# An eight-layer linear-attention block with a mixture of ten units, one Trainium2 core: the mixture's down product in plain f32

## What is computed

```python
scores = jax.nn.softmax(xf @ router_w, axis=-1)
topk_scores, topk_idx = jax.lax.top_k(scores, TOP_K)
combine = jnp.zeros((N, E), dtype=x.dtype).at[jnp.arange(N)[:, None], topk_idx].add(topk_scores)
g = jnp.einsum('nh,ehf->enf', xf, gate_w)
u = jnp.einsum('nh,ehf->enf', xf, up_w)
y = jnp.einsum('enf,efh->enh', jax.nn.silu(g) * u, down_w)
routed = jnp.einsum('enh,ne->nh', y, combine)
shared = jax.nn.silu(xf @ shared_gate_w) * (xf @ shared_up_w) @ shared_down_w
x = x + gb * (shared + routed)
```

## Time and profile before

| | |
|---|---|
| runs | 521.98, 522.12, 523.74 us, median 522.12 |
| profiled execution | 523.33 us, its span 521.3 us |
| PE busy | 505.4 us, 97% of the span |
| DVE, ACT, POOL busy | 425.6, 404.2, 294.5 us |
| granted PE clock, mean | 0.993 |
| the mixture, steps 2 to 39 | 414.8 to 517 us of the span |

### The profile page before, as it was taken

One profiled execution on the slowest core, in us unless ns is written; L12 is line 12 of the kernel. 1 busy time (PEld: TensorE's weight loads), 2 busy tenths in 40 slices (PEclk: granted clock), 3 DMA queues, 4 the chain that ended last, 5 costly groups with the idle time before them and its releaser, 6 DMA issues.

```text
span 521.3 us, 8267 instructions
## 1 busy us (share of the span) xinstructions
PE 505.4 (97%) x1993; PEld 310.4 (60%) x1993; DVE 425.6 (82%) x1631; ACT 404.2 (78%) x606; POOL 294.5 (56%) x328
## 2 busy tenths in 40 slices
PE   8789999999999999999999999999989999899997
PEld 6445555555555555555555555555555568687885
DVE  5879888988898888888888988888886667877754
ACT  3848888888888888888888888888887866657552
POOL 4435655556656566655566555666545567555652
PEclk8989999999999999999999999999999999999999
DMA  8200010001000000100010001001000000000000
GB/s 242 97 16 1 7 41 15 0 5 40 15 5 20 20 15 5 41 15 0 5 40 15 5 4 36 15 5 29 12 1 1 2 0 1 21 1 21 2 21 20
DMA packets 16070, 11.22 MB, mean 22 GB/s; under 512 B 8220, under 2 KB 13852, under 8 KB 16052
## 3 DMA queue, kind: packets, MB, share of 16 engines
q1 hardware_dynamic: 15188, 10.29, 7.1%
q10 hardware_dynamic: 864, 0.73, 0.5%
HBM read 9.96 MB, written 1.05 MB: 21 GB/s over the span
## 4 chain that ended last, share of the span: by engine, by line
PE 84%; DVE 6%; POOL 4%; issue 3%; ACT 2%; DMA 1%; DVEq 0%; POOLq 0%; ACTq 0%
PE bank L436 19%; PE bank L427 15%; PE bank L302 12%; PE bank L449 6%; PE bank L424 5%; PE bank L344 4%; PE bank L349 4%; PE bank L345 4%; PE bank L546 3%; PE bank L548 3%; PE bank L547 3%; PE bank L591 1%; PE bank L594 1%; PE bank L592 1%; PE bank L606 1%
## 5 line engine op out<-in xcount | busy, mean ns | idle before, releaser
L436 PE MATMUL bank<-hid,wf 128*128 128x512 f32 x256 | 120.2, 592 | 0.0
L917 POOL TENSOR_TENSOR rsD<-veD,c_half 128x4 f32<-128x4 f32 x32 | 37.3, 1166 | 100.7 <-DVE veD L1031 100.7
L427 PE MATMUL bank<-x,wf 128*128 128x512 f32 x192 | 93.9, 598 | 0.0
L755 ACT ACTIVATE hid<-bank,vbf 128x512 f32<-128x512 f32 x128 | 77.6, 694 | 1.9 <-PE bank L427 1.9
L436 PEld LDWEIGHTS bank<-hid,wf 128*128 128x128 f32 x256 | 46.0, 190 | 46.6 <-issue 30.8
L1002 POOL TENSOR_TENSOR xs_lo<-sc,xs_hi 128x512 fp32r<-128x512 f32 x36 | 46.6, 1296 | 41.4 <-ACT xs_hi L875 41.3
L427 PEld LDWEIGHTS bank<-x,wf 128*128 128x128 f32 x192 | 35.4, 191 | 33.7 <-issue 16.5
L1121 DVE TENSOR_SCALAR x<-bank,vln 128x256 f32<-128x256 f32 x64 | 31.9, 540 | 23.8 <-PE bank L302 23.8
L1050 DVE TENSOR_SCALAR xhB<-bank,meanB,rsB 128x128 f32<-128x128 f32 x128 | 43.8, 407 | 9.2 <-POOL rsB L917 9.2
L1050 DVE TENSOR_SCALAR xhD<-bank,meanD,rsD 128x128 f32<-128x128 f32 x128 | 43.7, 406 | 7.4 <-POOL rsD L917 3.2
L725 ACT ACTIVATE g<-bank,vbf 128x512 f32<-128x512 f32 x31 | 21.4, 691 | 35.5 <-PE bank L436 35.5
(11 more groups left out here) (173 smaller groups left out, 1178.7 us busy)
## 6 DMA issues: line engine op xcount, KB each, us to landing
wf<-in_w_f SPq DMA_DIRECT2D x16, 256.0 KB, 2.7
wu<-in_w_unit SPq DMA_DIRECT2D x10, 192.0 KB
wqkv<-in_w_qkv SPq DMA_DIRECT2D x7, 192.0 KB, 2.3
x<-in_x SPq DMA_DIRECT2D x4, 256.0 KB, 5.5
out<-ot SPq DMA_DIRECT2D x3, 256.0 KB, 2.2
wo<-in_w_o SPq DMA_DIRECT2D x8, 64.0 KB, 1.8
wmod<-in_w_mod ACTq DMA_DIRECT2D x1, 256.0 KB, 5.6
vln<-in_v_ln SPq DMA_DIRECT2D x16, 1.0 KB, 1.7
```

The costliest lines, as they stand in the source:

```text
L427: mm = nc.tensor.matmul(ps_ff[j][:], wf1[:, j * P:(j + 1) * P], x2[(c - 2) % CH][:], start=True, stop=True)
L436: mm = nc.tensor.matmul(ps_f0[:], wf2[:, j, :], hid[:, j, :], start=(j == 0), stop=(j == FJ - 1))
L755: nc.scalar.activation(hid[:, j, :], ps_ff[j][:], ACT.Gelu_apprx_tanh, bias=vbf1[:, j:j + 1]).then_inc(h_ready, 1)
L917: nc.gpsimd.tensor_tensor(rs[buf(k, n)][:], ve[buf(k, n)][:], c_half[:], ALU.pow).then_inc(rstd_ready[k], 1)
```

## The change

The down product of every step is one plain f32 matmul of `wu` and the unit's result `sc` itself. `sc_hi`, `sc_lo`, ACT's rounding, POOL's subtraction, `splits` and the waits that belong to them go. `wu_hi` and `wu_lo` are made for the gate and up matrices only (128x256 in place of 128x384). POOL's last four weight parts, which stood behind the low parts of steps 2, 4, 5 and 7, stand at steps 2 to 5. The slots that drain the layers keep their order.

```diff
-                if splits(i + 1) == splits(i):
-                    unit_done(pe, i)
-                    mm = nc.tensor.matmul(ps_y[:], wu[:, u, 2, :], sc[i % 3][:], start=(u == 0), stop=(u == U - 1))
-                else:
-                    k = splits(i)
-                    pe.wait_ge(sc_hi_ready, k + 1)
-                    nc.tensor.matmul(ps_y[:], wu_hi[:, u, 2, :], sc_hi[k % 2][:], start=(u == 0), stop=False)
-                    nc.tensor.matmul(ps_y[:], wu_lo[:, u, 2, :], sc_hi[k % 2][:], start=False, stop=False)
-                    pe.wait_ge(sc_lo_ready, k + 1)
-                    mm = nc.tensor.matmul(ps_y[:], wu_hi[:, u, 2, :], sc_lo[k % 2][:], start=False, stop=(u == U - 1))
+                unit_done(pe, i)
+                mm = nc.tensor.matmul(ps_y[:], wu[:, u, 2, :], sc[i % 3][:], start=(u == 0), stop=(u == U - 1))
...
-                    nc.scalar.activation(wu_hi[:, u, :, :], wu[:, u, :, :], ACT.Copy).then_inc(wu_hi_ready, 1)
+                    nc.scalar.activation(wu_hi[:, u, 0:2, :], wu[:, u, 0:2, :], ACT.Copy).then_inc(wu_hi_ready, 1)
...
-                if splits(i) > splits(i - 1):
-
-                    k = splits(i - 1)
-                    unit_done(act, i - 1)
-                    if k >= 2:
-                        act.wait_ge(down_mm, i - 2)
-                        act.wait_ge(sc_lo_ready, k - 1)
-                    nc.scalar.activation(sc_hi[k % 2][:], sc[(i - 1) % 3][:], ACT.Copy).then_inc(sc_hi_ready, 1)
...
-                    nc.gpsimd.tensor_tensor(wu_lo[:, u, :, :], wu[:, u, :, :], wu_hi[:, u, :, :].bitcast(F32),
+                    nc.gpsimd.tensor_tensor(wu_lo[:, u, 0:2, :], wu[:, u, 0:2, :], wu_hi[:, u, 0:2, :].bitcast(F32),
                                             ALU.subtract).then_inc(wu_lo_ready, 1)
 
-            LATE_LOW = {0: 6, 2: 7, 3: 8, 5: 9}
+            LATE_LOW = {0: 6, 1: 7, 2: 8, 3: 9}
...
-                k = splits(i)
-                pool.wait_ge(sc_hi_ready, k + 1)
-                if k >= 2:
-                    pool.wait_ge(down_mm, i - 1)
-                nc.gpsimd.tensor_tensor(sc_lo[k % 2][:], sc[i % 3][:], sc_hi[k % 2][:].bitcast(F32),
-                                        ALU.subtract).then_inc(sc_lo_ready, 1)
-                if k in LATE_LOW:
-                    split_weights_lo(ORDER[LATE_LOW[k]:LATE_LOW[k] + 1])
+                if i - FIRST in LATE_LOW:
+                    split_weights_lo(ORDER[LATE_LOW[i - FIRST]:LATE_LOW[i - FIRST] + 1])
...
                 if i >= 3:
                     dve.wait_ge(down_mm, i - 2)
-                    if splits(i - 2) > splits(i - 3):
-                        dve.wait_ge(sc_lo_ready, splits(i - 2))
```

More of the change, by code:

```diff
@@ L104, in adaln_block @@
         sc = [sb(f"sc{i}", [P, G]) for i in range(3)]
-        sc_hi, sc_lo = xs_hi[2:], xs_lo[2:]
         yf = sb("yf", [P, G])
@@ L158, in adaln_block @@
         sg_ready, su_ready, sc_ready = sem("sg_ready"), sem("su_ready"), sem("sc_ready")
-        sc_hi_ready, sc_lo_ready = sem("sc_hi_ready"), sem("sc_lo_ready")
         yf_ready, out_tm, ot_ready = sem("yf_ready"), sem("out_tm"), sem("ot_ready")
@@ L201, in run @@
                 extra[place]()
-        def splits(i):
-            return min(max(i - FIRST, 0), CH * U - FIRST - 2)
         def unit_done(eng, i):
```

## The result

The changed kernel takes 525.04 us (median of five runs, 524.68 to 526.26) against 522.13 us (five runs) before: a ratio of 1.005, 95% interval 1.0035 to 1.0066. It is 2.9 us slower; 524.8 was predicted, +2.7. The profiled execution took 524.68 us, its span is 522.8 us. So the two profiles differ by 1.35 us only, and the reason lies ahead of the mixture, in nothing that was changed. The transposes of chunk 0's rows (`xhF`) start at 403.17 us before and at 401.99 after.

The account below looks back on a forecast made before the run. PE was taken to bound the kernel, busy 505.4 of 521.3 us. Its added work of +5.8 us less 3.1 us of waits gave +2.7, so 522.12 us would become 524.8, range 523.3 to 527.0 us.

Parts of the forecast that it names:

- +5.8 us from one row: PE's down product and broadcast: 1.09 us plain against 0.93 split, 0.16 us more in each of 36 steps.
- The bounds: Limits of PE's added work: +4.7 us at 0.13 us a step, up to +9.7 us at 0.27.
- both dearer rivals: PE's plain product: format-change price, 528.7 us, chance 0.06; four passes at full price of four fp32r matmuls, 527.4 us, 0.06.
- 1.30 + 0.3 + 0.83 + 0.28: Waits to go: broadcasts of steps 4, 14, 24; their restarts; transposes of step 5 (425.29); transposes at 453.90, in us.
- The step that named ACT's rounding at 453.90: Transposes wait for ACT to empty `ps_v` behind a rounding; without it ACT starts at 452.71, not 452.99: 0.28 us gained.
- The broadcasts' 1.6 us: Waits at steps 4, 14, 24, 1.30 us plus 0.3 for restarts, end once POOL's low parts no longer hold DVE.
- The hold of DVE by POOL: Tiny 128x4 DVE operations take 1.15 or 1.30 us, not 0.16, ending when POOL's low-part subtraction ends.
- That offset: The earlier profiled execution lay 1.2 us above the median; its forecast went from 523.33 to 526.0 us.
- All of the waiting goes: Rival: lighter ACT also removes the remaining 1.2 us at 453.90 and 0.2 at 410.49; +1.3, 523.4 us; chance 0.16.
- the wait at 410 us: Transposes at 410.49 wait for POOL's power behind one weight part; the narrower part gains 0.3 us.
- Another cause: Rival: DVE's long operations aren't due to POOL and stay, three broadcasts still wait; +4.3, 526.4 us; chance 0.08.
- the two halves: Main case, cut at 0.5% (2.6 us): with rivals, slower by over 0.5% has 0.51, within 0.5% has 0.45.

Follow-up runs that it names:

- e1: Kernel before with its split down products, but without ACT's roundings and POOL's low parts (old buffer contents read): 519.14 us, 0.9939 of before.
- e4: Split kernel without roundings and low parts, with a fourth fp32r matmul added to each of the 36 down products: 528.04 us.
- e3: Kernel before with plain down products, ACT's 36 roundings kept but unread, POOL's low parts left out, weight parts still 128x384: 525.08 us.
- e5: Kernel before, but POOL's low part of unit 2 (steps 2, 12, 22) covers 4 of 512 columns: 520.55 us, 0.9965 of before.
- e2: Kernel before with plain f32 down products in all 40 steps, while ACT and POOL still make the unread rounded and low parts: 527.28 us.
- e6: Kernel before, but POOL's low part of unit 4 (steps 4, 14, 24) covers 4 of 512 columns: 522.42 us, 1.0002 of before.
- e10: Changed kernel plus one unread POOL subtraction of 128x512 SBUF data at the start of the variance in chunks 0 to 2: 527.04 us.
- e11: Changed kernel plus one unread POOL memset of 128x512, reading nothing from SBUF, at the start of the variance in chunks 0 to 2: 525.48 us.
- e8: Kernel before with plain down products at steps 2, 12, 22 and 14, and POOL's third weight part moved behind the power: 520.15 us.
- e9: Kernel before with plain down products at steps 2, 12, 22 and POOL's weight parts moved off the first routing and the power: 519.84 us.
- e7: Kernel before with plain down products at steps 2, 12 and 22 only, without rounding or low part there: 519.96 us, 0.9952 of before.

## Why the prediction was right, and where it was not

**PE's work: right.** +5.8 us from one row was +5.87 in the comparison of the changed kernel with e1. The bounds and both dearer rivals are settled: there is no price at the change of format (1.09 us wherever fp32r matmuls stand on both sides; and behind other work the difference is the same, as at step 6, where the router, the down product and the broadcast take 1.98 us after and 1.82 before), and four single passes cost 2.84 us more than the plain product.

The count that the Trainium skill gives in "FP8 and Floating Point Precision", "TensorE Precision Notes", four passes for true FP32, is no price of four single matmuls: 0.86 us against 0.94 in e4.

**The waits: right in the sum, partly wrong in the reasons.** 3.1 us were to go. The front gave 11.60 - 11.32 = 0.28 us (0.3 predicted). The stretch gave 5.87 - (104.41 - 101.43) = 2.89 us; my terms for it were 1.30 + 0.3 + 0.83 + 0.28 = 2.7. Term by term, in e1 beside the kernel before, the broadcasts gave 1.31 us, the restarts and the transposes of step 5 together 1.14, the transposes of step 15 0.29, and smaller pieces the rest.

- *The step that named ACT's rounding at 453.90 failed.* The gain there is as large as forecast, 1.25 to 0.96 in the bracket, but e3 keeps the rounding and has it too, and e5 as well, with all roundings. The whole queue of ACT was late at that place. Before, an earlier rounding waited for DVE's held result, and from it ACT worked without a gap up to the emptying of the bank at 452.99:

```profile
449.86 0.63 ACT L875 ACTIVATE xs_hi<-sc 128x512 fp32r<-128x512 f32 x1 [1.23 <-DVE sc L1337]
```

  DVE was late because of POOL. I read the instruction ahead in the queue as the cause, when the queue was only passing a delay on. What taking the roundings away would give while POOL's low parts stay, no run shows.
- *The broadcasts' 1.6 us were put to the hold alone.* A slower PE would have taken 1.0 us of waiting by itself (e2). I priced the two terms one by one from the profile of before and added them; they overlap, and the sum came right all the same, because the hold's removal takes away whatever is left.
- *The hold of DVE by POOL* was read from two pairs of ends that agree to 0.02 us. e5, e6, e10 and e11 show it by experiment: the right three operations of 36, made narrow, give 1.9 us; three others give none; one put back in each of three chunks holds DVE again.

**The sum: right.** From the `xhF` transposes to the end of the stretch the profile grew by -0.28 + 2.98 = +2.70 us, the figure forecast, while the medians differ by 2.9. The profiled execution did not go to 526.0 us but to 524.68, since the earlier profile had lost 1.2 us at a lower clock before 40 us. That offset should have been left out of its forecast.

**The rivals.** "All of the waiting goes" fell: 0.96 us of the bracket at step 15 stay, with and without ACT's rounding, so a lighter ACT doesn't remove them. Of the wait at 410 us, 0.49, the forecast 0.3 went (0.28) and 0.21 stayed, as assumed in the sum; it went whole where the third weight part doesn't stand ahead of the power (e8 and e9, front 11.1 us). "Another cause" fell with e5 and e10.

**Chances.** The bound of 0.5% is 2.6 us, the result is 2.9, with an interval from 0.35% to 0.66%. The interval holds 0.5% itself, so the measurement doesn't decide between the two halves either: 0.51 against 0.45 was as near as this sum could tell, and that the median lies on the likelier side is in part luck.

## What to carry to other kernels

On a PE that is the bound, price a change of number format by the pitch from start to start in a row where both formats stand side by side: here one 128x512 f32 matmul is 0.86 us, three fp32r ones are 0.70, four 0.94. Relief of an engine that isn't the bound pays only where a wait of the bound leads back to it, and there a few instructions may carry the whole gain: three plain down products out of 36 gave 2.5 us (e7), all 36 cost 2.9. A tiny DVE operation that takes as long as a POOL operation beside it is held by it; look for such pairs before moving work to or on POOL, since a moved operation takes its hold along (e5, e8, e9).

## What was unexpected of the hardware

- Making a POOL operation short doesn't free DVE where another stands behind it: in e5 the next one started 0.15 us after the short one, and the variance took 1.02 us.
- A copy with a single SBUF input (CAST to fp32r, 128x32) took 1.26 us beside a POOL subtraction in e9 and 0.18 in e7: held were not only operations with two inputs.
- PE pays about 0.1 us when a 128x512 fp32r matmul starts behind a wait: 0.33 to 0.35 us to the next start in place of 0.23 (and again in e2, 422.44 to 422.78). No wait is needed for it: behind a group of 128x128 transposes or the router's matmuls it is 0.31 to 0.33 us each time in the mixture before (425.70 to 426.02, for one), and behind the clean plain product it isn't there.
